# Attention probabilities in steps of four heads for narrow tiles, with the order of events set anew

## What is computed

```
q, k = rotary(h @ Wq), rotary(h @ Wk)          # 32 heads of 16
a    = softmax(where(causal, q k^T * scale, NEG))
o    = a @ [v1, v2]                            # one pair of heads: o1 and o2
attn = lowpass(o1 - lambda_full * o2)          # along the sequence, rfft and irfft in the reference
attn = attn * rsqrt(mean(attn**2) + EPS) * rms_weight * (1 - LAMBDA_INIT)
x    = x + attn @ Wout
```

## Time and profile before

| | |
|---|---|
| time, median of 3 runs | 1260.25 us (1258.77 to 1263.32) |
| the profiled execution: its time | 1260.45 us |
| the profiled execution: its span | 1258.7 us |
| mean granted TensorE clock | 0.967 of full speed |
| busy in the span: PE, DVE, ACT, POOL | 90%, 64%, 49%, 64% |

### The profile page before, as it was taken

The page is one execution under the profiler, slowest core; times in us unless marked ns, Lnnn a source line. Parts: engine busy times, 40 slices in busy tenths (PEclk is TensorE's granted clock), DMA queues, the critical chain, the costliest instruction groups (busy, mean ns, idle before and its releaser), DMA issues. The chain is left out here.

```text
span 1258.7 us, 20791 instructions
## 1 busy us (share of the span) xinstructions
PE 1127.6 (90%) x7603; PEld 639.1 (51%) x7618; DVE 811.5 (64%) x1345; ACT 618.0 (49%) x1009; POOL 800.6 (64%) x584
## 2 busy tenths in 40 slices
PE   6999967989689889889898898897899999999996
PEld 5888722333234343343243243342367888887764
DVE  6887175565564665656557646643288788787786
ACT  4444215657557657656666564666642233332321
POOL 2012159569969879869879789668215677667321
PEclk9999959899889999999999998998999999999999
DMA  8333340120231220220221203103332322233651
GB/s 273 98 126 109 90 116 26 51 68 26 67 78 41 68 68 26 68 68 26 69 68 39 58 21 109 30 1 129 107 110 96 131 84 94 92 101 116 222 197 51
DMA packets 74836, 107.55 MB, mean 85 GB/s; under 512 B 12912, under 2 KB 36592, under 8 KB 74736
## 3 DMA queue, kind: packets, MB, share of 16 engines
q1 hardware_dynamic: 63616, 79.35, 21.4%
q0 software_dynamic: 4064, 14.16, 2.9%
q10 hardware_dynamic: 7056, 12.72, 2.7%
HBM read 68.44 MB, written 37.75 MB: 84 GB/s over the span
## 5 line engine op out<-in xcount | busy, mean ns | idle before, releaser
L1090 DVE TENSOR_REDUCE nm<-score 128x1 f32<-128x640 f32 (+6 forms) x352 | 349.4, 1025 | 272.6 <-PE score L981 220.8
L1257 POOL TENSOR_TENSOR base<-base,plain 128x2048 f32<-128x2048 f32 (+2 forms) x78 | 301.0, 3860 | 16.1 <-ACT plain L1206 6.2
L1206 ACT ACTIVATE plain<-score 128x1024 f32<-128x1024 f32 (+3 forms) x288 | 207.2, 734 | 108.4 <-PE score L997 60.4
L992 PE MATMUL score<-q,k 98*128 98x512 bf16 (+7 forms) x768 | 194.9, 340 | 51.7 <-ACT plain L1206 21.1
L992 PEld LDWEIGHTS score<-q,k 98*128 98x128 bf16 (+1 forms) x768 | 55.0, 99 | 155.1 <-DVE nm L1090 58.0
L1206 ACT ACTIVATE base<-score 128x1024 f32<-128x1024 f32 x96 | 97.5, 1023 | 72.9 <-PE score L997 51.6
L1010 PE MATMUL acc<-plain,vg 128*32 128x512 f32 (+3 forms) x1152 | 114.4, 470 | 0.0
L976 PE MATMUL score<-k,q 48*128 48x512 bf16 (+3 forms) x512 | 70.5, 355 | 17.7 <-DVE nm L1090 17.5
L1612 PE MATMUL m_b<-m_winh,m_hTh 128*128 128x512 f32 x192 | 83.6, 435 | 1.6 <-DVE m_k L1902 1.6
L1612 PE MATMUL m_b<-m_winh,m_hTl 128*128 128x512 f32 x192 | 75.8, 395 | 0.0
L1612 PE MATMUL m_b<-m_winl,m_hTh 128*128 128x512 f32 x192 | 75.7, 394 | 0.0
(11 more groups left out here) (312 smaller groups left out, 2514.3 us busy)
## 6 DMA issues: line engine op xcount, KB each, us to landing
q<-piece_scratch SPq DMA_DIRECT2D x192, 64.0 KB, 2.7
k<-piece_scratch SPq DMA_DIRECT2D x192, 64.0 KB, 2.3
piece_scratch<-n_pieces SPq DMA_DIRECT2D x16, 384.0 KB, 3.0
piece_scratch<-pieces POOLq DMA_DIRECT2D x8, 768.0 KB, 4.0
n_x1in<-in_query SPq DMA_DIRECT2D x16, 256.0 KB, 3.6
v_scratch<-n_v ACTq DMA_DIRECT2D x16, 256.0 KB, 2.2
vg<-v_scratch SPq DMA_DIRECT2D x8, 512.0 KB, 4.4
att_scratch<-m_qT SPq DMA_DIRECT2D x8, 512.0 KB, 3.0
```

The costliest lines, as they stand in the source:

```text
L992: mm = nc.tensor.matmul(score[k % RING][:, x, t0:HALF], kst[n % SLOTS][c, first + x, j * P:(j + 1) * P], qst[n % SLOTS][c, first + x, h * ...
L1090: nc.vector.tensor_reduce(out, src, AX.X, ALU.max, negate=True).then_inc(s_max, 1)
L1206: nc.scalar.activation(tile_of(n, v)[:, first:first + 2, t0:HALF], score[k % RING][:, :, t0:HALF], ACT.Exp)\
L1257: nc.gpsimd.tensor_tensor(total, total, tile_of(n, v)[:, :, t0:HALF], ALU.add)\
```

## The change

Where a tile has 256 or 128 queries (tiles 2, 3, 10 and 11), one probability step now holds all four heads: heads 0 and 1 lie side by side in the first bank, heads 2 and 3 in the second. One mask product then serves two heads, by a broadcast of the mask, and one exponential reads all four. A set has 20 probability steps instead of 24. All distances of the event list are set anew, and rotations start in other sets.

```diff
 def prob_steps():
-    return [(h, j, head) for h in range(2) for j in range((h + 1) * TB // 2) for head in (0, 2)]
+    steps = []
+    for h in range(2):
+        for j in range((h + 1) * TB // 2):
+            n = 2 if (j + 1) * P - h * HALF <= HALF // 2 else 4
+            steps += [(h, j, range(first, first + n)) for first in range(0, GH, n)]
+    return steps
...
-EVAC_LATER = {'turn': 0, 'low': 0, 'square': 3, 'shift': 0, 'den': 0}
-VALUES_LATER, DEN_LATER, OUT_LATER, NUM_LATER = 3, 3, 4, 1
-ADD_LATER = {'dve': 3, 'pool': 0}
-PIECES_LATER, SUMS_LATER, MISC_FREE = 4, 8, 2
+EVAC_LATER = {'turn': 1, 'low': 0, 'square': 0, 'shift': 1, 'den': 0}
+VALUES_LATER, DEN_LATER, OUT_LATER, NUM_LATER = 2, 1, 8, 0
+ADD_LATER = {'dve': 0, 'pool': 1}
+PIECES_LATER, SUMS_LATER, MISC_FREE = 4, 4, 1
...
-TURNED_IN, SWAP_AT = (0, 2, 3, 4, 6, 8, 10, 12), 3
+TURNED_IN, SWAP_AT = (0, 1, 2, 3, 5, 7, 9, 11), 10
...
-                for x in range(2):
-                    c = FULL[x]
-                    mm = nc.tensor.matmul(score[k % RING][:, x, t0:HALF], kst[n % SLOTS][c, first + x, j * P:(j + 1) * P],
-                                          qst[n % SLOTS][c, first + x, h * HALF + t0:(h + 1) * HALF], start=True,
-                                          stop=not diag, skip_group_check=True)
+                diag, width, each = j >= 4 * h, HALF - t0, len(heads) // 2
+                banks = [score[k % RING][:, x, 0:each * width].rearrange("p (a t) -> p a t", a=each) for x in range(2)]
+                for y in range(each):
+                    for x in range(2):
+                        head = heads[each * x + y]
+                        c = FULL[head % 2]
+                        mm = nc.tensor.matmul(banks[x][:, y], kst[n % SLOTS][c, head, j * P:(j + 1) * P],
+                                              qst[n % SLOTS][c, head, h * HALF + t0:(h + 1) * HALF], start=(y == 0),
+                                              stop=not diag and y == each - 1, skip_group_check=True)
                 if diag:
+                    mask = mask_t[:].rearrange("p (o t) -> p o t", o=1).broadcast_to([P, each, P])
...
+                nc.scalar.activation(
+                    tile_of(n, v)[:, heads[0]:heads[-1] + 1, t0:HALF].rearrange("p (b a) t -> p b a t", a=each),
+                    score[k % RING][:, :, 0:each * (HALF - t0)].rearrange("p b (a t) -> p b a t", a=each), ACT.Exp)\
```

More of the change, by code:

```diff
@@ L612 @@
 NRU, NPU = len(RU), len(PU)
-NV = NPU // 2
+TILES = list(dict.fromkeys(u[:2] for u in PU))
+NV = len(TILES)
+LAST_OF = [max(m for m, u in enumerate(PU) if u[:2] == tile) for tile in TILES]
 FIRST_HALF = sum(1 for u in RU if u[0] < TB // 2)
@@ L631 @@
 ADDS = {e: [v for v in PLAIN if v in ADDED and ADDED[v][1] == e] for e in ("dve", "pool")}
-TERMS = [[v for v in range(NV) if v not in ADDED and PU[2 * v][0] == h] for h in range(2)]
+TERMS = [[v for v in range(NV) if v not in ADDED and TILES[v][0] == h] for h in range(2)]
 AT_ONCE, AT_END = [6, 7], [4, 8, 9, 10, 11]
@@ L810, in first_query @@
         def first_query(v):
[L811 removed]
+            h, j = TILES[v]
             return max(j * P - h * HALF, 0)
@@ L984, in probs @@
             def probs(n, m):
-                h, j, first = PU[m]
+                h, j, heads = PU[m]
                 k = place["probs", n, m]
@@ L1188, in prob_of @@
             def prob_of(n, m):
-                h, _, first = PU[m]
-                v, k, t0 = m // 2, place["probs", n, m], first_query(m // 2)
+                h, j, heads = PU[m]
+                v, k = TILES.index((h, j)), place["probs", n, m]
+                t0, each = first_query(v), len(heads) // 2
                 act.wait_ge(s_unit, k + 1)
@@ L1204, in prob_of @@
                         else:
-                            act.wait_ge(s_misc, order["den", bn, PU[2 * bv][0]])
-                nc.scalar.activation(tile_of(n, v)[:, first:first + 2, t0:HALF], score[k % RING][:, :, t0:HALF], ACT.Exp)\
+                            act.wait_ge(s_misc, order["den", bn, TILES[bv][0]])
+                nc.scalar.activation(
+                    tile_of(n, v)[:, heads[0]:heads[-1] + 1, t0:HALF].rearrange("p (b a) t -> p b a t", a=each),
+                    score[k % RING][:, :, 0:each * (HALF - t0)].rearrange("p b (a t) -> p b a t", a=each), ACT.Exp)\
                     .then_inc(s_exp, 1)
```

20 lines of the change are left out of this document (9 added, 11 removed).

## The result

After the change the kernel takes 1252.91 us (median of 6 runs, 1250.99 to 1254.81). Before it took 1261.53 us in the same comparison (6 runs, 1258.77 to 1263.86). The ratio is 0.9949, with a 95% interval of 0.9932 to 0.9966: faster by 0.5%, where 1.7% was forecast. The profiled execution took 1250.99 us with a span of 1249.2 us, 9.5 us less than before, where the prediction's sum has 21 us.

The account below looks back on a forecast made before the run. POOL was taken to set the pace, in even sets 3.1 us ahead of PE. Even sets -36, odd +19.6, set 0 -3.6, set 13 -1.6, set 14 -1.9, 2.5 put back: -21 from 1260.45 gives 1239.5 us, range 1222 to 1262.

Parts of the forecast that it names:

- a wait for tile 5 in even sets: Sign of being right: POOL newly waits for ACT's tile 5 in even sets, 40 to 55 us in the stage.
- The new place of the rotation: Three rotation operations, 7.2 us, move ahead of tile 5 in odd sets 5, 7, 9, 11: 4.9 us longer each.
- the price of nothing for DVE's additions: DVE's additions of tiles 9 and 10 begin about when POOL's addition of tile 7 ends, and cost nothing.
- 25.8: Even sets: tile 5 comes 25.8 us after T, the end of POOL's addition of tile 7, instead of 26.3.
- 47.6 us: Length of an even set before the change, read from set 8; forecast to fall to 41.6 us.
- The merges: Two merged steps ahead of tile 5 in an even set, with the freed ring steps: 0.8 us saved, between 0 and 2.
- Set 13 was to give 1.6 us: Set 13 loses PE's 3.19 us wait for the stacked operands and its own rotation: 44.5 us instead of 46.1.
- what would make it wrong: Sign of being wrong, without a size: the denominators hold PE for the addition of tile 2.
- The output at T + 7.4 instead of 6.5: Even sets: the output comes 6.5 us after POOL's addition of tile 7 ends, instead of 11.0 before.
- PE is later at tile 5: Rival: in even sets, waits for the bank `misc` make PE late ahead of tile 5; 1270 us; chance 0.11.
- DVE meets POOL: Rival: in seven odd sets DVE's additions fall into POOL's unbroken chain, 16 to 24 us; 1256 to 1264 us; chance 0.15.
- Nothing moves: Rival: POOL's work stays the same, and odd sets pay what even sets save; 1256 to 1262 us; chance 0.09.

Follow-up runs that it names:

- Experiment 3: The changed kernel with the second and third parts of a rotation at distances 34 and 40 instead of 17 and 34: 1249.77 us.
- rotation_in_hole: The changed kernel with the rotations of sets 5, 7, 9, 11 started one set earlier, their long operations behind the even set's addition of tile 2: 1251.86 us.
- experiments 2 and 6: Merged steps done with two exponentials and four mask products: in the changed kernel 1252.02 us; in the one with odd-set products later and rotation moved (1236.02 us), 1236.20 us.
- experiment 5: The changed kernel with rotations moved into even sets, 1251.86 us; the same with the first half's denominators four steps later in all sets, 1270.51 us.
- odd_later: The changed kernel with, in odd sets only, the first half's denominators and the next set's first shift four steps later, behind tile 5's scores: 1244.35 us.

## Why the prediction was wrong

**Right.** The direction, and the move of the bound: POOL's wait for `rden` gave way to a wait for tile 5 in even sets, of the size forecast. The new place of the rotation cost what was said (4.9 us for an odd set forecast, 5.0 measured). PE's wait for the stacked operands is gone from set 13, and POOL's additions kept their 4.5 us.

**The step that failed** is the price of nothing for DVE's additions: "I see them begin at about T, where POOL waits for `rden` anyway: cost nothing". They began there, and POOL itself lost nothing. But PE's denominators wait for them, and POOL's moved rotation operation held the second of them up. PE stood for 1.90 us, and tile 5 came at T + 27.6 instead of 25.8 in sets 8 and 10. Experiment 3 shows the price where PE is equally far at T: 42.5 us with the collision, 41.1 without it. In sets 2, 4 and 6 it is smaller: the second group of the denominators begins at T + 5.1, and at T + 4.5 in sets 6, 8 and 10 of `rotation_in_hole`, where nothing collides and the sets last 42.2 us, 0.7 less.

**What the sum left out: the granted clock.** The prediction took 47.6 us as the length of an even set from set 8, in which the clock was low right after T; at full clock it was 46.4, so that 2.4 of the 10 us that the even sets lack were never there in sets 6 and 10. After the change the six even sets last 257.5 us together, against 249.6 forecast and 246.6 at 41.1 each. By the rows above, an estimate, the 10.9 us over 41.1 are 6.3 of collision (three sets with 1.4 us, three with 0.7), 3.3 for PE late at T in sets 2, 4 and 6, behind odd sets in which the clock fell, and 1.3 for the low clock in set 12.

**Mis-sized terms.** The merges were counted at 0.8 us for an even set; their instructions are worth nothing (experiments 2 and 6), and the step of the ring that each frees was not tried alone. That 25.8 without them came so near to the 26.2 of experiment 3 is partly luck: PE's two waits for `misc`, 1.3 us, stand in that path too, where the prediction had 0.4 us for them. Set 13 was to give 1.6 us and gave nothing: PE's wait for the operands was replaced by one for POOL's addition of tile 2, and the clock that fell behind it took another 1.1 us. The prediction had named that wait as what would make it wrong, and had not priced it. The output at T + 7.4 instead of 6.5 is the collision again: it comes at T + 5.7 in experiment 3, behind set 5. The list of POOL's waits left out another 14.5 us for `rden`, at an operation of the even sets' outputs.

**Right number, half the cause.** The odd sets' 5 us were put on POOL's rotation. It is one of two bounds that lie beside one another. Taking it away gave nothing (experiment 5, where the clock fell as well), taking PE's two waits for POOL away gave nothing (experiment 6, `odd_later`), and both together gave 3.5 us a set.

**The rivals.** "PE is later at tile 5" had the right place. Its mechanism, the bank `misc`, holds PE for 1.3 us in an even set, but giving the bank more time costs 40 us. "DVE meets POOL" happens, at T, with DVE and then PE as the payers. "Nothing moves" fell: sets moved by 5 us each, in both directions.

## What to carry to other kernels

A collision is not free because the engine that it slows is waiting: ask what that engine waits for, and whether the slowed work is on the way there. Where a set keeps its length when its obvious bound is taken away, look for a second bound at the same place, and take both away before judging either. Before the length of one set goes into a sum, look at its granted clock: here six sets of the same kind were of two lengths, 1.3 us apart. Distances counted in steps belong to one layout of steps: the new steps alone and the new distances alone made the kernel 8% and 13% slower, and the pair made it 0.5% faster.

## What the runs showed of the hardware

The granted clock fell right after some of PE's waits, and stayed after others, and the length of the wait alone didn't decide it. Behind waits of 1.41 to 1.45 us at the same place of the odd set it was 1.00, 0.64, 0.50 and 1.00 (experiment 3); behind one of 1.68 us in set 13 of the change it fell, and behind one of 1.65 us in set 13 of `rotation_in_hole` it stayed. Two more windows, of set 13 of the change and, behind a wait of 1.64 us, of set 9 of `rotation_in_hole`:

```profile
780.00:786.00 6.00, 5.97 (x46) 1.89 (x46) 2.25 (x3) 3.01 (x4) 0.35 (x2) 0.76 0.45 111
...
602.50:606.00 3.50, 3.47 (x26) 1.35 (x27) 0.20 (x1) 1.01 (x2) 2.40 (x3) 0.51 0.51 140
```

The second is the lower of the two levels, 1.2 GHz, and the first half's denominators take 1.94 us there instead of 1.06. By an estimate from this row, 3.5 us at half the clock are 1.7 us of products lost, about as much again as the wait. What it costs a set is 1.1 us in set 13, where PE is the bound (46.4 against 45.3 us), and nothing in set 7 of experiment 3, where POOL is; there the next set pays.
